# Attention kernel: row sum matmul ahead of the P times V block, outputs multiplied from PSUM, POOL's additions in halves, and DVE's side work in other slots

## The reference

```python
B, N, D, H, DK = 8, 1024, 256, 16, 64
xn = layernorm(x)
q, k, v = (heads(xn @ W.T + b) for W, b in ((Wq, bq), (Wk, bk), (Wv, bv)))
att = softmax(einsum('bhqd,bhkd->bhqk', q, k) / sqrt(DK))
out = heads_joined(einsum('bhqk,bhkd->bhqd', att, v)) @ Wo.T + bo
routed = moe(xn)      # 64 experts, top 8, up to 128 rows of an expert: silu(g) * u @ w_down
return x + out + routed + shared_ffn(xn)
```

## Time and profile before

| | us |
|---|---|
| median of 3 runs | 3772.88 |
| lowest and highest of them | 3740.12, 3776.08 |
| time of the profiled execution | 3781.51 |
| its span (first to last instruction) | 3779.8 |
| TensorE busy | 3555.8 (94%) |
| DVE busy | 2904.5 (77%) |
| POOL busy | 2604.9 (69%) |
| ACT busy | 1764.7 (47%) |

### The profile page before, as it was taken

The page is one execution under the profiler, slowest core; times in us unless marked ns, Lnnn a source line. Parts: engine busy times, 40 slices in busy tenths (PEclk is TensorE's granted clock), DMA queues, the critical chain, the costliest instruction groups (busy, mean ns, idle before and its releaser), DMA issues. The chain is left out here.

```text
span 3779.8 us, 58889 instructions
## 1 busy us (share of the span) xinstructions
PE 3555.8 (94%) x16232; PEld 2093.8 (55%) x16232; DVE 2904.5 (77%) x3190; ACT 1764.7 (47%) x3254; POOL 2604.9 (69%) x1426
## 2 busy tenths in 40 slices
PE   7999579999999999999999999999999999999899
PEld 6777345555555555555555555555555555555487
DVE  7888558788788878888888887888888778788544
ACT  4444234444444444444444444444444444444443
POOL 1111148888888888888888887888888888888611
PEclk9999789999999999999999999999999999999899
DMA  7766455666666666666665666666666666664286
GB/s 220 222 204 199 138 130 124 164 163 161 166 161 163 167 162 162 161 162 161 161 162 160 160 161 161 165 165 165 165 165 165 165 165 165 165 165 121 97 311 232
DMA packets 393626, 635.53 MB, mean 168 GB/s; under 512 B 48048, under 2 KB 214640, under 8 KB 393584
## 3 DMA queue, kind: packets, MB, share of 16 engines
q1 hardware_dynamic: 370800, 603.54, 58.1%
q0 software_dynamic: 14336, 23.08, 2.9%
q10 hardware_dynamic: 8448, 8.39, 0.6%
HBM read 306.91 MB, written 126.12 MB: 115 GB/s over the span
## 5 line engine op out<-in xcount | busy, mean ns | idle before, releaser
L1214 POOL TENSOR_TENSOR sums<-sums,probs 128x1024 f32<-128x1024 f32 x768 | 1842.9, 2400 | 237.6 <-ACT probs L1053 186.9
L1092 DVE TENSOR_REDUCE merged<-psum 128x1 f32<-128x1024 f32 x1024 | 1201.4, 1215 | 416.1 <-PE psum L918 416.1
L1053 ACT ACTIVATE probs<-psum 128x512 f32<-128x512 f32 x2048 | 1084.2, 600 | 723.1 <-PE psum L892 721.3
L933 PE MATMUL psum<-probs,v_sb 128*64 128x512 f32 x4096 | 935.2, 599 | 0.0
L889 PE MATMUL psum<-q_full,k_full 128*128 128x512 f32 x2048 | 879.7, 430 | 0.0
L892 PE MATMUL psum<-q_rest,k_rest 65*128 65x512 f32 x2048 | 813.9, 397 | 0.0
L933 PEld LDWEIGHTS psum<-probs,v_sb 128*64 128x64 f32 x4096 | 271.5, 136 | 532.1 <-issue 440.1
L965 PE MATMUL psum<-x_t,w_qk 128*128 128x512 f32 x1536 | 424.4, 412 | 138.9 <-DVE merged L1092 103.6
L889 PEld LDWEIGHTS psum<-q_full,k_full 128*128 128x128 f32 x2048 | 389.4, 190 | 196.3 <-issue 94.7
L1214 POOL TENSOR_TENSOR sums<-probs 128x1024 f32<-128x1024 f32 x128 | 305.8, 2389 | 276.8 <-ACT probs L1053 275.1
L1121 DVE RECIPROCAL sum_all<-sum_all 128x128 f32<-128x128 f32 x512 | 479.1, 937 | 19.5 <-ACT sum_all L1063 19.5
(11 more groups left out here) (142 smaller groups left out, 3133.9 us busy)
## 6 DMA issues: line engine op xcount, KB each, us to landing
x_t<-xt SPq DMA_DIRECT2D x118, 1024.0 KB, 8.1
k_full<-high SPq DMA_DIRECT2D x256, 256.0 KB
v<-values SPq DMA_DIRECT2D x64, 512.0 KB, 3.2
w_qk<-wqk_parts SPq DMA_DIRECT2D x64, 512.0 KB, 3.4
q_full<-high SPq DMA_DIRECT2D x128, 256.0 KB
q_full<-low SPq DMA_DIRECT2D x128, 256.0 KB
k_rest<-low SPq DMA_DIRECT2D x128, 256.0 KB
q_rest<-high SPq DMA_DIRECT2D x128, 256.0 KB
```

The costliest lines, as they stand in the source:

```text
L933: last = nc.tensor.matmul(out_ps[rows, :], v_sb[:, par, kt, rows], probs[:, kt, h, :], start=(kt == 0), stop=(kt == KT - 1))
L1053: nc.scalar.activation(probs[:, kt, h, :], ring[ring_place(g, j) % RING], ACT.Exp, scale=SCALE).then_inc(probs_ready, 1)
L1092: nc.vector.tensor_reduce(out=merged[:, col:col + 1], in_=work[:, 2 * h:2 * h + 2, :].rearrange("p b c -> p (b c)"), axis=AX, op=ALU.max, ...
L1214: nc.gpsimd.tensor_tensor(sums[:, half, :, :], first, probs[:, kt, :, :], ALU.add).then_inc(sums_added, 1)
```

## The change

Five edits, made together. TensorE: in slots 0 and 2 `add_up` stands ahead of `pv`. ACT: the copy of the output bank goes; it copies the row sums only. DVE: OUT reads the output bank itself, and `pv` waits for OUT (`out_ready`) before it writes the bank again; SILU1 becomes two reciprocals of 128 columns, SILU1 and SILU2; the fillers stand in other slots, with OUT1 of the pair before in slot 1 and OUT0 of the same pair in slot 3. POOL: each addition becomes two, one for each head, with 512 columns. SP: the two stores follow the new order of OUT.

```diff
-FILLERS = ((("RECIP02",), ("RECIP03",), ("TOKEN0", "TOKEN1", "TOKEN2")),
-           (("OUT0",), ("RECIP10",), ("SILU0", "RECIP11")),
-           (("RECIP12",), ("RECIP13",), ("SILU1",)),
-           (("OUT1",), ("RECIP00",), ("RECIP01",)))
+FILLERS = (((), (), ("RECIP10", "RECIP11")),
+           (("RECIP12", "RECIP13"), ("OUT1",), ("TOKEN0", "TOKEN1", "TOKEN2")),
+           (("SILU0", "SILU1"), ("SILU2",), ("RECIP00", "RECIP01")),
+           (("RECIP02", "RECIP03"), ("OUT0",), ()))
...
             if gg % 2 == 0 and not known(2 * p + gg // 2, 1):
-                pe.wait_ge(out_copied, 2 * p + gg // 2)
+                pe.wait_ge(out_ready, 2 * p + gg // 2)
...
                 if g == 0 and fin:
+                    add_up(s, 1, fin)
                     pv(s - 1, 1 - par, SLOTS - 1)
-                    add_up(s, 1, fin)
+                if g == 2 and att:
+                    add_up(s, 0, fin)
                 if g > 0 and att:
                     pv(s, par, g - 1)
-                if g == 2 and att:
-                    add_up(s, 0, fin)
...
         def empty(p, half):
 
-            act.wait_ge(pv_done, 4 * p + 2 * half + 2)
+            act.wait_ge(sum_filled, 2 * p + half + 1)
             if not known(p, 1):
-                act.wait_ge(out_stored[half], DMA * p)
-            nc.scalar.copy(out_raw[:, half, :], out_ps).then_inc(out_copied, 1)
-            act.wait_ge(sum_filled, 2 * p + half + 1)
+                act.wait_ge(out_ready, 2 * p - 1 + half)
             nc.scalar.copy(sum_all[:, half, :], ring[SUM_PLACE[half] % RING]).then_inc(sum_copied, 1)
...
-                dve.wait_ge(recip_ready, 8 * s - 4 + 4 * half)
-                dve.wait_ge(out_copied, 2 * (s - 1) + half + 1)
-                nc.vector.tensor_tensor(out_raw[:, half, :], out_raw[:, half, :], sum_all[:, half, :], ALU.mult
+                if not (fin if half else att):
+                    return
+                p = s - half
+                dve.wait_ge(recip_ready, 8 * p + 4 * half + 4)
+                dve.wait_ge(pv_done, 4 * p + 2 * half + 2)
+                if not known(p, 1):
+                    dve.wait_ge(out_stored[half], DMA * p)
+                nc.vector.tensor_tensor(out_raw[:, half, :], out_ps, sum_all[:, half, :], ALU.mult
                                         ).then_inc(out_ready, 1)
...
-                dve.wait_ge(silu_vec, 2 * s + 1)
-                nc.vector.reciprocal(silu[:], silu[:]).then_inc(silu_vec, 1)
+                dve.wait_ge(silu_vec, 3 * s + 1)
+                cols = slice((n - 1) * P, n * P)
+                nc.vector.reciprocal(silu[:, cols], silu[:, cols]).then_inc(silu_vec, 1)
...
-                    nc.gpsimd.tensor_tensor(sums[:, half, :, :], first, probs[:, kt, :, :], ALU.add
+                    nc.gpsimd.tensor_tensor(sums[:, half, 0, :], first[:, 0, :], probs[:, kt, 0, :], ALU.add)
+                    nc.gpsimd.tensor_tensor(sums[:, half, 1, :], first[:, 1, :], probs[:, kt, 1, :], ALU.add
                                             ).then_inc(sums_added, 1)
```

More of the change, by code:

```diff
@@ L842, in attention_stage @@
     pv_done = sem("pv_done")
-    out_copied = sem("out_copied")
     sums_added = sem("sums_added")
@@ L1113, in filler @@
                 half, n = int(name[-2]), int(name[-1])
-                late = name in ("RECIP02", "RECIP03") or half == 1
-                if not (fin if late else att):
+                if not (fin if half else att):
                     return
-                p = s - 1 if late else s
+                p = s - half
                 if n == 0:
@@ L1121, in filler @@
                 nc.vector.reciprocal(sum_all[:, half, cols], sum_all[:, half, cols]).then_inc(recip_ready, 1)
-            elif name.startswith("OUT") and fin:
+            elif name.startswith("OUT"):
                 half = int(name[-1])
-                dve.wait_ge(recip_ready, 8 * s - 4 + 4 * half)
-                dve.wait_ge(out_copied, 2 * (s - 1) + half + 1)
-                nc.vector.tensor_tensor(out_raw[:, half, :], out_raw[:, half, :], sum_all[:, half, :], ALU.mult
+                if not (fin if half else att):
+                    return
+                p = s - half
+                dve.wait_ge(recip_ready, 8 * p + 4 * half + 4)
[3 more added lines that the diff above has]
+                nc.vector.tensor_tensor(out_raw[:, half, :], out_ps, sum_all[:, half, :], ALU.mult
                                         ).then_inc(out_ready, 1)
@@ L1199, in step @@
                     if (half, kt) == (1, GROUP):
-                        pool.wait_ge(silu_vec, 2 * s + 2)
+                        pool.wait_ge(silu_vec, 3 * s + 3)
                         nc.gpsimd.tensor_tensor(silu[:], up_gate[:, P:3 * P], silu[:], ALU.mult).then_inc(gated, 1)
@@ L1309, in step @@
             if fin:
-                store(s - 1, 0)
+                store(s - 1, 1)
             if nxt:
                 shift_out(s + 1, pp, 0)
-            if fin:
-                store(s - 1, 1)
+            if att:
+                store(s, 0)
             if loads:
```

## The result

Against the kernel before in the same set of runs (3770.93 us median of 4, 3740.12 to 3776.08) the changed kernel takes **3651.42 us** median of 4, 3649.46 to 3653.55: ratio 0.9677, interval 0.9649 to 0.9706. The profiled execution took 3649.46, with a span of 3647.7.

A forecast was written before the change was run, and what follows sets the result against it. TensorE, with two waits a step behind DVE, was taken as the bound. The profiled 3781.5 less 127 (60 x 2.08 = 125, first step 2) plus 2 gave 3656; between that and 3648 it said 3654 us, range 3640 to 3672, chance 0.62.

The forecast's parts named there:

- The bound and the saving: TensorE's two waits a step, before the projections of slots 1 and 2: 60 steps at 45.67 instead of 47.75 save 125 us.
- one floor for all runs: Runs differ in how often steps are free of waits; without waits all reach the same time, 3656 down to 3648.
- The fillers' places: DVE's fillers in each slot's third place overrun behind POOL instructions; new places fit gaps of 2.8 and 1.97 us.
- TOKENs in slot 1: Slot 1, third place: DMA wait goes, three TOKENs take 1.0 to 2.3 us, middle 1.65, of 1.97; at worst 0.3 a step.
- OUT from PSUM: DVE multiplies from the output bank: 0.74 us instead of mostly 2.65, bounds 0.7 to 2.7; cost 0.
- Row sums first: TensorE's sum matmul ahead of P times V, 3.5 us earlier, without meeting an unfinished POOL sum; cost 0.
- POOL: Halved additions cost 0.18 us more each, 2.5 a step, bounds 0.1 to 0.77; 4.0 idle us take it.
- (a): DVE gets in only after both POOL halves, so one wait a step stays: 65 us back, 3719; chance 0.19.
- (b): POOL sets the step if an instruction's fixed cost exceeds 0.29 us: 3840 at 0.5, about 4065 at 0.77; chance 0.06.
- (c): New TensorE wait, for OUT before P times V or slot 2's low part: 84 us back, 3740; chance 0.06.
- (d): DVE's fillers don't make TensorE's waits, so nothing changes: 3775 us; chance 0.04.

The follow-up runs named there:

- group 1: The changed kernel with POOL's additions whole again: 3710.10 us, ratio 0.9826.
- group 2: The changed kernel with the sum matmul behind P times V again, in both slots: 3886.76 us, ratio 1.0299.

## Why the prediction was right, and where it wasn't

**The bound and the saving.** Right. It was TensorE's two waits; the steps without them measured the prize beforehand (45.67 us), and the 60 steps now take 45.62 in the mean: 128 us saved, 125 predicted. That a wait costs more than its length held too: 0.88 shown, 1.04 reckoned, and 128 us over the 110 waits of these steps are 1.16 each. The very number, 3654 for 3651.42, owes something to luck: the sum for the profiled execution was 3656, which took 3649.46, 3 us less by the steps and 4 by the last part of the run, and 3654 was a choice between that sum and 3648. The presumption behind that choice, one floor for all runs, fits: the four runs of the changed kernel lie within 4 us, those of the kernel before within 36.

**The fillers' places.** Right in effect, with one step wrong in cause. The prediction took the two waits for two separate causes, TOKEN0's in slot 0 and SILU0's in slot 1, each from standing behind a POOL instruction (with 1.47 us of DMA wait in one of them), and read both long durations as what is to be shortened. The runs show one root, DVE's delay in slot 0: taking away its DMA wait alone frees both PJs (3644.96), putting an equal delay back restores both (3771.61), and halving POOL's instructions alone gives nothing (3771.48). SILU0's 2.4 us came from the moment at which it asked, and that moment was set by the first wait. The prediction's own held the hint: in the steps without waits SILU0 took 0.28 with whole additions on POOL. The change cures the root by asking for the counts a slot later; it would have been as well cured by issuing their DMA earlier. That the change hit both waits by treating each of them is in part luck: it treated the root among others.

**TOKENs in slot 1.** 1.0 to 2.3 us were allowed; they take 1.0 in nearly all steps (0.28 + 0.29 + 0.27 and the gaps), not 1.65. That halves are needed for it is right: with whole additions TOKEN0 takes 2.367 there and 0.75 us of wait comes in each step (group 1).

**OUT from PSUM.** 0.74 predicted, 0.68 measured, cost 0 as said; it gives no time either, with OUT back in SBUF 3648.66. By the cycle table of the Trainium skill (VectorE: DVE Perf Modes, the section on the TRN2 errata) the source in PSUM should add; these runs don't show it like for like: behind the same low part OUT takes 0.68 us from PSUM, and 0.68 from SBUF in every other case of the kernel with the copy; behind an idle stretch it takes 0.691 to 0.693 from PSUM in the changed kernel, and 0.693 from SBUF in the kernel before. (The least seen from SBUF is 0.622, once in a run, behind a reciprocal.) The low part (L1100), from which "the trace agrees in direction" was taken, isn't the same operation, so that reading was too weak.

**Row sums first.** Cost 0, right: POOL ends the first half's sum at 2040.92 and the second's at 2018.42, 5.3 and 5.0 us ahead of their sum matmuls, more than the 4 expected. What the prediction left out is the price of doing without them (235 us, group 2); it says only that the reciprocals "need the row sums copied".

**POOL.** 0.18 us more per addition was predicted, 0.13 measured (2.58 against 2.45 from start to start), since a second half starts 1.23 behind the first though that lasts 1.28. POOL keeps 3.1 idle us, not 1.5. The last part of the run, from the last PJ on, was to cost 2 us more; it takes 317.6 against 319.8, 2.2 less. With whole additions it takes 316.0, so the halves cost 1.6 there, as said, and the other edits, which the prediction put at nothing, give 3.8.

**The rivals.** (a), one wait stays: its mechanism exists, but for OUT alone; TOKEN0 and SILU0, with one tensor source, took 1.42 us at most in all kernels with halves. What I set against it, that OUT never exceeds 3.209, said nothing, since the kernel before had no two additions on POOL without a wait between them. (b) was not reached, and its threshold is borne out: POOL was to set the step from 0.29 us more per addition on, and it does so with the wait between the halves, at 2.76 - 2.45 = 0.31. (c) didn't come: TensorE waits neither for OUT nor for the low part in the steady steps (the waits without early sums are of another kind, for the reductions). (d) fell with the result, but the halves alone would have borne it out.

## What to carry to other kernels

When an engine waits twice in a cycle, delay or free one place on purpose before treating both: two waits with different names can have one root, and the second can be a matter of phase against a third engine. An instruction that seems slow because another engine holds it may only be asking at the wrong moment; steps of the same kernel in which it is short show this without a run. An operand that a slow indirect DMA brings is best issued a half step early or asked for a slot later. The first was worth 3.4% here by itself. The second was not run by itself; within the change it carries 91 of the 120 us. And an edit has no price of its own (the halves: 0 alone, 59 us gained in one company, 12 lost in another).

## What was not expected of the hardware

A DVE instruction with two sources in SBUF stands for both of two POOL instructions issued without a wait between them (3.06 us for the row above, 3.942 at most), while one with a single tensor source gets in after the first (TOKEN0 1.20 us, asked 0.17 after a half began); with a semaphore wait between, two sources get in too (1.772 at most). The Trainium skill (SBUF — State Buffer, the section SBUF: two separate sides) says that the two engines share a pair of ports as an exclusive lock, which the first gets "for the whole instruction", and names DVE instructions with two SBUF inputs among those that need it. That OUT from PSUM never exceeds 0.693 agrees with that; these runs add that two POOL instructions can hold DVE off as one.

Some waits of TensorE are followed by a longer PJ, others of the same length are not. Over the last 60 steps of all kept runs, 401 waits of up to 1.14 us left the next PJ at 1.68 us or less; behind 178 waits of 1.29 to 2.31 us it took 1.82 to 2.93 us in 55 cases and 1.74 at most in the other 123. The one shown, 2.78 us behind 1.38, goes with a granted clock of 0.75 and 0.83 in the windows around. The mean granted clock of the profiled runs goes the same way, 0.984 changed, 0.975 with the halves alone, 0.973 with the sums behind.

The indirect DMA of the counts, 128 columns wide, landed 6.6 us behind its issue in the kernel before (2035.57 to 2042.17), and 6.4 and 7.6 us in two steps in a row of the kernel with the halves alone (2025.06 to 2031.43, 2071.74 to 2079.34); over the run of the kernel before it is 5.6 to 8.2. Runs of the kernels in which a wait hangs on this DMA spread by more: 18 us (3758 to 3776) with the halves alone, 33 (3724 to 3757) with the tokens back, 12 to 36 in the sets of the kernel before, and 8 at most where nothing waits for it.
